# Routing steps of VectorE, list writes of GpSimd and the first weight splits in another order, in an attention and mixture-of-experts block

## What is computed

```
def attention(q, latent, Wq, Wkv, Wout):          # 16 heads of 32
    k, v = split(latent @ Wkv.T)
    scores = (q @ Wq.T heads) . (k heads) / sqrt(32), masked causally
    return (softmax(scores) @ v) @ Wout.T

def ffn(x, gate_w, fc1, fc2, proj, shared...):    # 8 experts of 352, 2 chosen per row
    probs = softmax(x @ gate_w.T); top_p, top_i = top_k(probs, 2)
    y  = sum over the two: top_p * (silu(x @ fc1[e].T) * (x @ fc2[e].T)) @ proj[e].T
    y += sigmoid(x @ shared_gate.T) * ((silu(x @ s1.T) * (x @ s2.T)) @ sp.T)   # 1408 wide
    return y

x = x + attention(layernorm(x), ctx, ...)
x = x + ffn(layernorm(x), ...)
```

## Time and profile before

| | us |
|---|---|
| median of 3 runs | 1514.06 |
| the runs | 1513.85, 1514.06, 1518.33 |
| the profiled execution | 1515.46 |
| its span, first to last instruction | 1513.7 |

### The profile page before, as it was taken

The page is one execution under the profiler, slowest core; times in us unless marked ns, Lnnn a source line. Parts: engine busy times, 40 slices in busy tenths (PEclk is TensorE's granted clock), DMA queues, the critical chain, the costliest instruction groups (busy, mean ns, idle before and its releaser), DMA issues.

```text
span 1513.7 us, 28281 instructions
## 1 busy us (share of the span) xinstructions
PE 1480.5 (98%) x10026; PEld 1257.8 (83%) x10026; DVE 860.0 (57%) x1460; ACT 653.2 (43%) x1836; POOL 586.8 (39%) x503
## 2 busy tenths in 40 slices
PE   6999999999889999999999999999999999999999
PEld 5888888888678899999999999887888888888887
DVE  5566776777765587876877867455223332233322
ACT  5999998999854323323323323332112121111211
POOL 3333456555552387685865864102100001000010
PEclk9999999999999999999999999999999999999999
DMA  7244466555375589767877764553203022030210
GB/s 244 67 118 117 104 125 94 123 108 124 65 155 111 155 324 329 270 251 264 282 244 267 275 222 170 176 207 86 95 15 112 28 67 61 12 111 28 63 49 28
DMA packets 102905, 217.44 MB, mean 144 GB/s; under 512 B 43696, under 2 KB 48816, under 8 KB 98064
## 3 DMA queue, kind: packets, MB, share of 16 engines
q1 hardware_dynamic: 91184, 184.71, 40.0%
q0 software_dynamic: 11616, 31.35, 7.1%
HBM read 168.86 MB, written 47.17 MB: 143 GB/s over the span
## 4 chain that ended last, share of the span: by engine, by line
PE 70%; issue 1%; DVE 1%; DMA 0%; POOL 0%; ACT 0%; POOLq 0%; DVEq 0%; ACTq 0%
PE psum L823 53%; PE psum L1142 11%; PE psum L902 2%; PE psum L1044 2%; PE psum L1068 1%; DMA routed<-expert_out_dram,slot_b 0%; DVE base L2007 0%; DVE base L2046 0%; DVE nT_lo L1942 0%; PE psum L1009 0%; POOL routed L1552 0%; PE psum L980 0%; POOL rs L1417 0%; PE psum L971 0%; DVE h_s L2019 0%
## 5 line engine op out<-in xcount | busy, mean ns | idle before, releaser
L1552 POOL DMA_INDIRECT routed<-expert_out_dram,slot_b x56 | 56.3, 1006 | 480.3 <-DVE slot_b L2001 327.8
L1247 ACT ACTIVATE probs<-psum,minus_max,rs 112x112 f32<-112x112 f32 x512 | 222.2, 503 | 3.8 <-DVE minus_max L1681 3.7
L2019 DVE TENSOR_TENSOR h_s<-psum,silu_s 128x512 f32<-128x512 f32 x66 | 45.7, 692 | 303.0 <-PE psum L823 303.0
L823 PE MATMUL psum<-nT_hi,ws_hi 128*128 128x512 f32 x528 | 209.6, 397 | 3.3 <-DVE nT_lo L1942 3.0
L823 PE MATMUL psum<-nT_lo,ws_hi 128*128 128x512 f32 x528 | 209.2, 396 | 0.0
L823 PE MATMUL psum<-nT_hi,ws_lo 128*128 128x512 f32 x528 | 209.1, 396 | 0.0
L1524 POOL DMA_INDIRECT xg<-normed_dram,tile_ids x63 | 150.0, 2381 | 35.6 <-DMA tile_ids<-lists_dram 13.3
L823 PE MATMUL psum<-wj_hi,gT_hi 128*128 128x352 f32 x504 | 162.8, 323 | 0.0
L823 PE MATMUL psum<-wj_hi,gT_lo 128*128 128x352 f32 x504 | 162.3, 322 | 0.0
L823 PE MATMUL psum<-wj_lo,gT_hi 128*128 128x352 f32 x504 | 161.8, 321 | 0.0
L1367 ACT ACTIVATE silu_s<-psum 128x512 f32<-128x512 f32 x66 | 39.4, 598 | 243.9 <-PE psum L823 243.9
(11 more groups left out here) (253 smaller groups left out, 3437.5 us busy)
## 6 DMA issues: line engine op xcount, KB each, us to landing
wj_raw<-in_w_experts SPq DMA_DIRECT2D x35, 1408.0 KB, 6.6
wj_raw<-in_w_experts SPq DMA_DIRECT2D x35, 768.0 KB, 5.7
wj_raw<-in_w_shared SPq DMA_DIRECT2D x22, 768.0 KB, 5.7
expert_out_dram<-y_c SPq DMA_DIRECT2D x63, 256.0 KB, 3.3
base<-x_dram SPq DMA_DIRECT2D x8, 1024.0 KB, 5.7
xT_raw<-in_xT SPq DMA_DIRECT2D x32, 224.0 KB, 4.8
x_in<-in_x SPq DMA_DIRECT2D x32, 224.0 KB, 4.7
x_res<-in_x SPq DMA_DIRECT2D x32, 224.0 KB, 4.8
```

The source lines that it names most:

```text
L823: mm = pe.matmul(out_ap, u, v, start=(n == 0), stop=(n == last))
L1247: done = act.activation(probs[:, j % 2, 4 * r + m, :], psum[0:SEQ, r, m * SEQ:(m + 1) * SEQ], ACT.Exp, bias=minus_max[:, r, m:m + 1], scal ...
L1552: pool.indirect_dma_start(out=routed[:, b % 2, c, :], out_offset=None, in_=expert_out_dram, in_offset=bass.IndirectOffsetOnAxis(ap=slot_b[ ...
L2019: dve.tensor_tensor(h_s[:, :], bank(b), silu_s[:, :], ALU.mult).then_inc(emptied_b[b], 1)
```

## The change

Four things are put in another order; but for two small edits (the means in halves, and the list writes two by two) nothing is added or taken away.

1. Start-up: the key and value weights are loaded second, and their high part is made first on ScalarE; the means are made in two halves in two banks, so that each half of the query weights is centred by itself; VectorE centres the first half, and then splits.
2. GpSimd writes the lists two by two over the four steps of a group, right behind `rinv_wide` and ahead of the context split and the roots. From batch 25 on rows are normalised one step later, right behind `rinv_wide`.
3. SyncE stores the routes in the first step of the next group, behind the store of the transposed rows.
4. VectorE does `choices` one step later, behind `rows_copy`, in groups 2 to 6 and for the placement that now falls into the first step of group 7; the rest of group 7 stays as it was.

```
@@ SyncE @@
             sp.dma_start(WEIGHTS[1][1], WEIGHTS[1][0]).then_inc(w_loaded[1], 16)
+            sp.dma_start(WEIGHTS[0][1], WEIGHTS[0][0]).then_inc(w_loaded[0], 16)
             sp.dma_start(ctx_in[:, :], ctxT[0]).then_inc(S["ctx_loaded"], 16)
...
-            sp.dma_start(WEIGHTS[0][1], WEIGHTS[0][0]).then_inc(w_loaded[0], 16)
...
+            def store_routes(n):
+                sp.wait_ge(S["slots_ready"], n)
+                sp.dma_start(route_rows[n - 1], route_of(n)[:, :, :]).then_inc(S["route_stored"], 16)
...
+                    if j == 0 and 3 <= g <= NG:
+                        store_routes(g - 2)
...
-                if routes(g):
-                    sp.wait_ge(S["slots_ready"], g - 1)
-                    sp.dma_start(route_rows[bass.ds(g - 2, 1)].rearrange("a s b f -> (a s) b f"),
-                                 route_of(g - 1)[:, :, :]).then_inc(S["route_stored"], 16)
+                if g >= NG:
+                    store_routes(g - 1)
@@ TensorE, weight_means @@
-                for k in range(KC):
-                    mm = pe.matmul(bank(0), mean_f[:, :], wq_raw[:, k, :], start=(k == 0), stop=(k == KC - 1))
-                mm.then_inc(S["mean_step"], 1)
+                for i in range(2):
+                    cols = slice(i * C // 2, (i + 1) * C // 2)
+                    for k in range(KC):
+                        mm = pe.matmul(bank(i, P, C // 2), mean_f[:, :], wq_raw[:, k, cols], start=(k == 0), stop=(k == KC - 1))
+                    mm.then_inc(S["mean_step"], 1)
@@ ScalarE, first_front @@
+                weights_hi(0)
                 for t in range(2):
                     x_hi(t)
-                weights_hi(0)
@@ GpSimd @@
+            def rows(t):
+                n, b = t + 1, t % 2
+                inverse_root(mv2, rs2, b, "stats2", "rstd2_made", n)
+                if t >= 2:
+                    wait_filled(pool, (t + 1) // TB, (t + 1) % TB, "normT")
+                    pool.wait_ge(xn2_stored[b], 16 * (t // 2))
...
+            FROM = (NG - 1) * TB - 3
...
+                    if there(g, j, 3) and t - 3 >= FROM:
+                        rows(t - 3)
+                    if 3 <= g < NG + 1:
+                        if j == 0:
+                            if g == 3:
+                                pool.wait_ge(S["lists_zeroed"], 16)
+                            else:
+                                move_ids(g - 3)
+                        scatter(g - 2, ITEMS[2 * j:2 * j + 2])
                     if j == 0 and before(g, NG):
                         split_context(2 * g + 2, g, 1)
                     if j == 2 and before(g, NG - 1):
                         split_context(2 * g + 3, g + 1, 0)
                     if there(g, j, -1):
                         scaled_root(t + 1)
-                    if routes(g - 1) and before(g, NG + 1):
...
-                        if j < 3:
-                            scatter(g - 2, ITEMS[3 * j:3 * j + 3])
...
+                    if there(g, j, 2) and t - 2 < FROM:
+                        rows(t - 2)
@@ VectorE @@
-                dve.wait_ge(S["mean_step"], 2)
-                dve.tensor_tensor(wq_raw[:, :, cols], wq_raw[:, :, cols], bank(0)[:, cols].unsqueeze(1).to_broadcast([P, KC, C // 2]),
+                dve.wait_ge(S["mean_step"], 2 + half)
+                dve.tensor_tensor(wq_raw[:, :, cols], wq_raw[:, :, cols], bank(half, P, C // 2).unsqueeze(1).to_broadcast([P, KC, C // 2]),
...
+            centre(0)
+            weights_lo(0)
             x_lo(0)
             x_lo(1)
-            weights_lo(0)
-            centre(0)
+            weights_lo(1)
             centre(1)
-            weights_lo(1)
             weights_lo(2)
...
-                if is_late(g) and (g == NG - 1 or (g == NG and j == 0)):
+                if (g == NG - 1 and j) or (g == NG and j == 0):
                     choices(*((g, j - 1) if j else (g - 1, TB - 1)))
...
                 if not is_late(g, 0):
                     rows_copy(g, j)
+                if t and (g < NG - 1 or (g == NG - 1 and j == 0)):
+                    choices(*((g, j - 1) if j else (g - 1, TB - 1)))
...
-                if is_late(g, 0) or not is_late(g, 2) or (j < TB - 1 and not is_late(g)):
+                if is_late(g, 0):
                     choices(g, j)
```

More of the change, by code:

```diff
@@ L1454, in _ @@
             late_consts()
+            def rows(t):
[4 more added lines that the diff above has]
+                    pool.wait_ge(xn2_stored[b], 16 * (t // 2))
+                pool.wait_ge(S["rstd2_made"], 2 * n)
+                settled(pool)
+                pool.tensor_scalar(xn2[:, b, :], x1[:, b, :], mv2[:, b, 0:1], rs2[:, b, 1:2], ALU.subtract, ALU.mult).then_inc(S["xn2_ready"], 1)
+            FROM = (NG - 1) * TB - 3
             def body(g):
```

14 lines of the change are left out of this document (removed).

## The result

| | before | after |
|---|---|---|
| median, us | 1515.07 | 1536.38 |
| the runs | 1513.85 to 1518.33 (4) | 1535.92 to 1537.46 (4) |
| span of the profiled execution | 1513.7 | 1534.3 |
| mean granted clock in it | 0.995 | 0.989 |

The ratio is 1.014, with a 95% interval of 1.0127 to 1.0154: the change makes the kernel 21 us slower. 1515.2 had been forecast, with 1520.5 as the upper end.

What follows compares the result with a forecast made beforehand. TensorE was taken as the bound, ScalarE's chain from batch 28 on. Terms -0.4 + 3.5 + 1.8 - 3.0 - 2.45 + 1.7 = +1.15 us on the median 1514.06 gave 1515.2, 8-in-10 range 1510.5 to 1520.5.

Steps and rivals of the forecast that it cites:

- Start-up: Before the first scores: VectorE begins centring when half of the sums are there; a gain, -0.4 us.
- Rank holes: Third steps of groups 2 to 6: second-expert chain delays attnT, so TensorE's rank products wait; +7.5 us in sum.
- First and second steps: First expert, second step: cost 0; placement, first step: GpSimd's list writes wait, 0.35 x 4 = 1.4 us, bounds 0 and 3.
- The clock, one dip: Behind group 7's new hole the granted clock drops once, 3.4 us at half speed, losing +1.7 us.
- Rival 3: Clock also drops behind the rank holes of groups 2 to 6, 1.7 us each: 1516.9 to 1523.7; two or more, chance 0.14.
- Group 7's first step: Keys of batch 28 wait for GpSimd's context split behind list writes: hole 2.8 us, +1.8, bounds 1.0 and 2.5.
- Step 29: `rinv_wide` now first on GpSimd, so the step falls from 14.17 to ScalarE's 11.17 us: -3.0.
- Step 32: `rinv_wide` now follows `rinv` instead of waiting for a row normalisation, so L960 begins at 427.3: -2.45 us.
- Route stores: SyncE's queue: only loads with a step to spare stand behind the moved stores, so cost 0.
- a load or store that I hold to be covered: Closing remark: besides the number of clock dips, what would most easily make the sum wrong; no size or chance given.

Runs made afterwards that it cites:

- part 2 alone: The kernel before with only GpSimd's new order; start-up, route stores and choices as before: median 1510.0 us, ratio 0.9967.
- the first experiment: The kernel after with VectorE's choices and placements put back where they stood before: median 1546.04 us, ratio 1.0199.
- parts 3 and 4 alone: The kernel before with only the later route stores and VectorE's choices one step later: median 1534.77 us, ratio 1.0122.

## Why the prediction was wrong, point by point

- **Start-up, -0.4.** It measures + 2 by itself (0.8 to 3.6 by the interval). The step that failed: the gain was followed to the first scores and not through the wait and the clock behind them. Even at the first scores the 1.3 us of the traces are a dip in the profiled run of before.
- **Rank holes, + 7.5.** Right: 7.9, with the releaser named. The chain took 2.92 us in the step shown (205.04 to 207.96) for my 2.6, and 2.55 to 3.01 in the five. Its first operation took 0.56 to 0.65 us in the three steps in which GpSimd's low part of the context ran beside it, and 0.18 and 0.20 in the other two (in the last the low part had ended 0.4 earlier). So only the split disturbs the new place, by 0.4 us. The Trainium skill's GPSIMD Engine Reference (Specifications), which the prediction cites, says that GpSimd contends for its SBUF interfaces with a VectorE instruction that has two SBUF inputs, as this one has; these five rows agree with it.
- **First and second steps, 0.35 a group, 1.4 in all.** In after the first steps of groups 3 to 6 took 13.0 to 13.2 us (a hole ahead of the keys) and the second steps 12.9 to 13.0 (a hole ahead of the inverse sums), against 12.4: 4.7 in all, above the bound of 3. Each was costed alone, while they hang together: in the kernel with the early context split these waits went and longer ones came in the third and fourth steps.
- **The clock, one dip, + 1.7.** This is the first term that failed. Rival 3, which had a chance of 0.14, was the mechanism: the clock fell at four of the five rank holes, 7.5 us by the trace and 7.0 by the kernel with the holes filled. The price of a dip was about right (1.5 for my 1.7, but 3.0 at the last hole); their number was not. The reason against it, that no dip followed holes of 0.5 to 1.4 in before, was read from few cases; here a dip followed a hole of 0.96.
- **Group 7's first step, + 1.8, with the dip 3.5.** Right in mechanism, 4.0 in size: hole 3.65 for 2.8, since placement ended at 398.8, 7.6 us into the step, and GpSimd began to write lists only 0.9 later. The dip came, but twice as long as counted, 6.8 us from 401.5 on: it began inside the hole and ran 1.8 us into step 29. With the 0.8 that it cost there the sum is 4.8 for my 3.5.
- **Step 29, -3.0.** -2.2 in after, where a dip of the clock runs into the step; exactly -3.0 in part 2 alone.
- **Step 32, -2.45.** Measured -2.45.
- **Route stores, 0.** This is the second term that failed, worth 8 us. I had asked who stands behind the store in SyncE's queue, and not who waits for its landing: VectorE's next first-expert chain writes the same buffer. In the groups the one-step-later chain had just enough room (no wait in after, 1.0 to 1.7 without part 2), at the end it had none. The rival "a load or store that I hold to be covered" was named only as a remark, with no place and no chance.

The sum failed on terms put at 1.7 (for one dip) and 0, which measure some 9 (7.5 at the rank holes and the rest at the hole of step 28) and 8. The account of the 20.6 us by the trace: in the groups + 15.4 (rank holes 7.9, their dips 7.5; the 4.7 us of first and second steps took the place of the 5.4 us of old holes), step 28 + 4.0, step 30 + 0.1, the last route store + 7.7, the stretch ahead of batch 8 - 2.0 (two dips in the trace of before and none in that of after, which is luck of the two profiled runs and not the start-up's worth), step 29 - 2.2, steps 31 and 32 - 2.45.

## What to carry to other kernels

- A store that is moved in one engine's queue has two neighbours: what is queued behind it, and who waits until its buffer is free. Cost both, above all in the last group, where the usual distance is missing; if it is short, a second buffer takes the wait away: here it gave back 33.5 of the 34 us of the first experiment.
- On an engine that bounds the kernel, price a hole with the clock that may fall behind it. Here that doubled the price, and work without use in the hole was cheaper than the hole.
- An experiment that undoes one of several linked moves can be worse than all of them. Undo in pairs, or take away the link first.

## What the runs showed of the hardware that I had not expected

- Six kernels here have five rank holes each. At all nine holes of 1.98 to 2.14 us the granted clock fell to its lower level of 1.2 GHz; at the 21 holes of 0.96 to 1.45 us it fell eleven times and stayed at 2.4 ten times, with 0.96 and 1.34 on both sides. So among these 21 the length of the hole alone doesn't settle it; what does is open.
- A route store of 12.2 KB released VectorE 8.5 us after its issue at the end of after (449.43 to 457.89) and 9.5 in parts 3 and 4 alone (184.00 to 193.47), behind three stores of 224 KB each on the same queue. Over the 27 such waits in eight kernels it was 4.9 to 9.5 us.
- The 20 runs of before on one chip spread from 1512.6 to 1518.6; their spans went with the mean granted clock, from 1510.8 at 0.997 to 1516.8 at 0.993. On another chip one run took 1510.8, its span 1509.1 at 0.999. A gain of 2 us needs many runs.
